# Context products of a cross-attention with high and low probabilities side by side, and the output weights' split one slot later

## What is computed

```python
q = rmsnorm((x @ Wq).reshape(b, s, 16, 128), gq)
k = rmsnorm((ctx @ Wk).reshape(b, 375, 16, 128), gk)
v = (ctx @ Wv).reshape(b, 375, 16, 128)
attn = softmax(einsum('bqhd,bkhd->bhqk', q, k) / sqrt(128))
out = einsum('bhqk,bkhd->bqhd', attn, v).reshape(b, s, 2048) @ Wo
```

## Time and profile before

| | |
|---|---|
| median of 3 runs | 1047.9 us |
| lowest and highest run | 1045.63 and 1049.46 us |
| profiled execution: its own time | 1046.03 us |
| profiled execution: span from first to last instruction | 1044.3 us |
| mean granted TensorE clock | 0.999 |

### The profile page before, as it was taken

The page is one execution under the profiler, slowest core; times in us unless marked ns, Lnnn a source line. Parts: engine busy times, 40 slices in busy tenths (PEclk is TensorE's granted clock), DMA queues, the critical chain, the costliest instruction groups (busy, mean ns, idle before and its releaser), DMA issues.

```text
span 1044.3 us, 20310 instructions
## 1 busy us (share of the span) xinstructions
PE 1018.9 (98%) x7021; PEld 910.0 (87%) x7021; DVE 722.6 (69%) x1496; ACT 536.6 (51%) x1075; POOL 532.7 (51%) x515
## 2 busy tenths in 40 slices
PE   8999999999999999999999999999999999999997
PEld 8856678999999999999999999999987888888885
DVE  4268876776767767767776776766886476666648
ACT  5355555555545455455555554554553356676610
POOL 1257767745534634643634634634474545544544
PEclk9999999999999999999999999999999999999999
DMA  8100114324333233323223233234220779999843
GB/s 279 83 32 2 61 39 153 143 109 157 116 108 114 99 107 111 101 109 116 96 111 115 94 117 109 98 118 136 98 90 1 286 282 386 387 393 399 294 119 113
DMA packets 45273, 153.46 MB, mean 147 GB/s; under 512 B 3768, under 2 KB 4792, under 8 KB 42144
## 3 DMA queue, kind: packets, MB, share of 16 engines
q1 hardware_dynamic: 42976, 145.38, 38.6%
q0 software_dynamic: 2240, 7.34, 2.1%
HBM read 130.04 MB, written 22.66 MB: 146 GB/s over the span
## 4 chain that ended last, share of the span: by engine, by line
PE 72%; POOL 5%; DVE 4%; issue 3%; ACT 1%; DMA 1%; POOLq 0%; DVEq 0%; ACTq 0%
PE xa_y_ps L86 6%; PE xa_y_ps L88 5%; PE xa_y_ps L87 5%; PE ex_raw_gu_ps L86 4%; PE ex_raw_gu_ps L88 4%; PE ex_raw_gu_ps L87 4%; PE xa_c_ps L1990 4%; PE xa_c_ps L1986 4%; PE xa_c_ps L1985 3%; PE ex_raw_ey_ps L2212 3%; PE xa_turn_ps L2067 3%; PE xa_turn_ps L2023 3%; PE front_k_ps L86 3%; PE front_k_ps L88 3%; PE front_k_ps L87 3%
## 5 line engine op out<-in xcount | busy, mean ns | idle before, releaser
L1300 POOL TENSOR_TENSOR xa_probs<-xa_probs,xa_inv_sum 112x750 f32<-112x750 f32 x63 | 97.9, 1553 | 75.5 <-DVE xa_inv_sum L1640 75.5
L1589 DVE TENSOR_TENSOR xa_kT_lo<-xa_turn_ps,xa_kT_hi 128x750 fp32r<-128x750 f32 x63 | 59.2, 939 | 99.9 <-ACT xa_kT_hi L1388 99.8
L1285 POOL TENSOR_TENSOR k_ms<-k_ss,sum_eps 125x6 f32<-125x6 f32 x63 | 12.6, 200 | 210.8 <-DVE k_ss L1605 210.8
L1985 PE MATMUL xa_c_ps<-xa_probsT_hi,xa_nat 125*128 125x224 f32 x384 | 92.3, 274 | 2.7 <-ACT xa_probsT_hi L1404 2.7
L1986 PE MATMUL xa_c_ps<-xa_probsT_hi,xa_nat 125*128 125x224 f32 x384 | 92.3, 275 | 0.0
L1404 ACT CAST xa_probsT_hi<-xa_turn_ps 125x672 fp32r<-125x672 f32 x62 | 44.6, 720 | 87.2 <-PE xa_turn_ps L2067 87.2
L1288 POOL TENSOR_TENSOR k_inv<-k_ms,neg_half 125x6 f32<-125x6 f32 x63 | 83.5, 1325 | 8.3 <-POOL k_ms L1285 6.7
L1410 ACT ACTIVATE xa_probs<-xa_scores_ps,xa_bias,xa_q_scale 112x375 f32<-112x375 f32 x126 | 82.8, 663 | 5.9 <-DVE xa_bias L1615 4.7
L1985 PEld LDWEIGHTS xa_c_ps<-xa_probsT_hi,xa_nat 125*128 125x128 f32 x384 | 73.6, 192 | 3.5 <-issue 3.1
L1986 PEld LDWEIGHTS xa_c_ps<-xa_probsT_hi,xa_nat 125*128 125x128 f32 x384 | 73.5, 191 | 0.5
L86 PE MATMUL front_k_ps<-land_xa_wk_hi,land_xa_ctx 128*125 128x256 f32 x252 | 71.4, 283 | 1.6 <-DVE front_k_hat L1632 1.2
(11 more groups left out here) (423 smaller groups left out, 3545.0 us busy)
## 6 DMA issues: line engine op xcount, KB each, us to landing
xa_nat<-ctx_split SPq DMA_DIRECT2D x56, 750.0 KB
ex_raw_raw<-in_w_units SPq DMA_DIRECT2D x15, 1408.0 KB, 8.2
ex_raw_raw<-in_w_units SPq DMA_DIRECT2D x15, 768.0 KB
land_ex_raw<-in_w_units SPq DMA_DIRECT2D x8, 1408.0 KB, 8.3
land_ex_raw<-in_w_units SPq DMA_DIRECT2D x8, 768.0 KB, 8.0
ctx_split<-xa_nat SPq DMA_DIRECT2D x8, 750.0 KB
sorted_x<-ex_raw_y_sb SPq DMA_DIRECT2D x7, 768.0 KB, 10.6
ex_raw_x_nat<-sorted_x SPq DMA_DIRECT2D x21, 256.0 KB, 8.6
```

The costliest lines, as they stand in the source:

```text
L1300: pool.tensor_tensor(probs[0:T, u % 2], probs[0:T, u % 2], inv_sum[0:T, u % 2, :].unsqueeze(2).broadcast_to([T, 2, KV]), ALU.mult).then_in ...
L1589: dve.tensor_tensor(kT_lo[:, :, 0:KV], turn_ps[:, :, 0:KV], kT_hi[:, :, 0:KV].bitcast(F32), ALU.subtract).then_inc(sem["kT_lo_done"], 1)
L1985: pe.matmul(c_view[:, c], nat[0:KT, u % 2, 0, at], probsT_hi[0:KT, :, cols], start=(t == 0), stop=False)
```

## The change

For batches u = 8 to 57 (`PAIRED`) high and low probabilities stand in one tile `probsT` beside each other, so that one matmul with nat high as weights takes both: 448 moving columns, of which 224 land in the first and 224 in the second half of a bank. Then three matmuls of 224 columns with nat low add to the first half. This takes a whole bank for each half c. The half c = 1 gets the second bank of `turn_ps`, in every paired batch; the half c = 0 has `c_ps` for itself in odd batches and is done so there, and in even batches stays as it was with nine matmuls ("three halves of four").

The sum of the two halves of a bank is now made late. ACT copies the first half as the high part (`cT_hi`, one copy for each c) and, for a paired half, the second half to `c_second`; DVE subtracts the high part from the first half into `c_rest`; POOL adds `c_rest` and `c_second` into `cT_lo`, as its first work in the slot. Since the second bank of `turn_ps` is used by the key transposes of the next slot, PE waits there, after the first keys, until DVE has read that bank (`second_bank_read`).

The output tile of each head pair's first sequence moves from slot 5 to slot 6 (`tile_of`), the rounding of the output weights moves on POOL behind `k_inv` of slot 4, their low part on DVE from the end of slot 4 to the start of slot 5, and the low part of the value weights on DVE from the end of slot 3 to the start of slot 4.

```diff
-        probsT_hi, probsT_lo = sb("probsT_hi", [P, 2, KT_N * T], F32R), sb("probsT_lo", [P, 2, KT_N * T], F32R)
+        probsT = sb("probsT", [P, 2, 2, KT_N * T], F32R)
+        probsT_hi, probsT_lo = probsT[:, 0], probsT[:, 1]
+        c_second = sb("c_second", [P, CC, 2, T])
+        c_rest = y_sb[:, 1, 0:CC * 2 * T].rearrange("p (c h t) -> p c h t", c=CC, h=2)
...
         def tile_of(u):
             b = u % B
-            return None if b == 1 else max(b - 1, 0)
+            return None if b == 0 else b - 1
...
+        c_pair = [bank[:, 0:4 * T].rearrange("p (l h t) -> p l h t", l=2, h=2) for bank in (c_ps, turn_ps[:, 1])]
+        PAIRED = range(B, N - B + 2)
+        def has_pair(u, c):
+            return c == 1 or u % 2 == 1
...
@@ POOL, slot @@
+                u = s - 3
+                if u in PAIRED:
+                    part = slice(u % 2 * T, (u % 2 + 1) * T)
+                    halves = slice(0 if has_pair(u, 0) else 1, CC)
+                    hold(pool, sem["c_rest_done"], i, CC * B, halves_read(u))
+                    pool.tensor_tensor(cT_lo[:, halves, :, part], c_rest[:, halves], c_second[:, halves],
+                                       ALU.add).then_inc(sem["cT_lo_done"], 1)
                 if s % B == 4 and s // B + 1 < PAIRS:
                     q = s // B + 1
                     split_hi(pool, i, q, "wq", wq_raw, wq_hi, "q_ready", 4, 4 * q)
...
-                if s % B == 4 and s // B < PAIRS:
-                    split_hi(pool, i, s // B, "wo", wo_raw, wo_hi, "y_ready", TILES, TILES * (s // B))
                 u = s
                 if u < N:
...
                     pool.tensor_tensor(k_inv[0:KT, :], k_ms[0:KT, :], env["neg_half"][0:KT, 0:2 * KT_N],
                                        ALU.pow).then_inc(sem["kinv_done"], 1)
+                if s % B == 4 and s // B < PAIRS:
+                    split_hi(pool, i, s // B, "wo", wo_raw, wo_hi, "y_ready", TILES, TILES * (s // B))
...
@@ ACT, slot @@
+                    for c in range(CC if u in PAIRED else 0):
+                        hold(act, sem["c_ready" if c else "c0_ready"], i, B, u + 1)
+                        act.copy(cT_hi[:, c, :, u % 2 * T:(u % 2 + 1) * T], c_pair[c][:, 0]).then_inc(sem["cT_hi_done"], 1)
+                        if has_pair(u, c):
+                            hold(act, sem["cT_lo_done"], i, B, u)
+                            act.copy(c_second[:, c], c_pair[c][:, 1]).then_inc(sem["c_second_done"], 1)
...
@@ DVE, slot @@
+                    for c in range(CC if u in PAIRED else 0):
+                        if has_pair(u, c):
+                            hold(dve, sem["c_second_done"], i, 3 * HALF, pairs_read(u, c))
+                            hold(dve, sem["cT_lo_done"], i, B, u)
+                        else:
+                            hold(dve, sem["cT_hi_done"], i, CC * B, CC * u + c + 1)
+                        dve.tensor_tensor(c_rest[:, c] if has_pair(u, c) else cT_lo[:, c, :, part], c_pair[c][:, 0],
+                                          cT_hi[:, c, :, part].bitcast(F32), ALU.subtract).then_inc(sem["c_rest_done"], 1)
+                if s % B == 4 and s // B < PAIRS:
+                    split_lo(dve, i, s // B, "wv", wv_raw, wv_hi, wv_lo)
+                if s % B == 5 and s // B < PAIRS:
+                    split_lo(dve, i, s // B, "wo", wo_raw, wo_hi, wo_lo)
...
-                if s % B == 3 and s // B < PAIRS:
-                    split_lo(dve, i, s // B, "wv", wv_raw, wv_hi, wv_lo)
-                if s % B == 4 and s // B < PAIRS:
-                    split_lo(dve, i, s // B, "wo", wo_raw, wo_hi, wo_lo)
...
@@ PE @@
+            def context_pairs(u, i):
+                context_loaded(u, i)
...
+                    hold(pe, sem["c_rest_done"], i, CC * B, halves_read(u - 1, 0))
+                hold(pe, sem["probsT_hi_done"], i, B, u + 1)
...
+                hold(pe, sem["probsT_lo_done"], i, B, u + 1)
+                for c in range(CC):
+                    if not has_pair(u, c):
+                        continue
+                    if c == 1:
+                        squares_taken(i, u + 2, 1)
+                    for t in range(KT_N):
+                        pe.matmul(c_pair[c], nat_part(u, 0, c, t), probsT[0:KT, :, :, cols[t]], start=(t == 0), stop=False)
+                    for t in range(KT_N):
+                        mm = pe.matmul(c_pair[c][:, 0], nat_part(u, 1, c, t), probsT_hi[0:KT, :, cols[t]], start=False,
+                                       stop=(t == KT_N - 1))
+                    mm.then_inc(sem["c_ready" if c else "c0_ready"], 1)
+            def second_bank_read(u, i):
+                hold(pe, sem["c_rest_done"], i, CC * B, halves_read(u))
...
@@ PE, slot: after the first keys, before the transposes of squares and keys @@
                     hold(pe, sem["probsT_lo_done"], i, B, u - 1)
                     squares_taken(i, s - 1, 1)
+                    if s - 3 in PAIRED:
+                        second_bank_read(s - 3, i)
                     turn_squares(i, s, 0)
```

More of the change, by code:

```diff
@@ L1577, in first_square_sums, with context_low @@
                                       ALU.add).then_inc(sem["qss_done"], 2)
+            def context_low(u):
+                part = slice(u % 2 * T, (u % 2 + 1) * T)
+                dve.wait_ge(sem["cT_hi_done"], CC * (u + 1))
+                dve.tensor_tensor(cT_lo[:, :, :, part], c_view, cT_hi[:, :, :, part].bitcast(F32),
+                                  ALU.subtract).then_inc(sem["cT_lo_done"], 1)
             def slot(s, i):
@@ L1581, in slot @@
                 if 0 <= u < N:
-                    hold(dve, sem["cT_hi_done"], i, B, u + 1)
                     part = slice(u % 2 * T, (u % 2 + 1) * T)
-                    dve.tensor_tensor(cT_lo[:, :, :, part], c_view, cT_hi[:, :, :, part].bitcast(F32),
-                                      ALU.subtract).then_inc(sem["cT_lo_done"], 1)
+                    if u not in PAIRED:
+                        context_low(u)
+                    for c in range(CC if u in PAIRED else 0):
[10 more added lines that the diff above has]
+                    split_lo(dve, i, s // B, "wo", wo_raw, wo_hi, wo_lo)
                 u = s - 1
@@ L1808, in combine @@
                                          in1=resid[:, t, :], op0=ALU.mult, op1=ALU.add).then_inc(xs["combined"], 1)
-            def context_low(u):
-                part = slice(u % 2 * T, (u % 2 + 1) * T)
-                dve.wait_ge(sem["cT_hi_done"], u + 1)
-                dve.tensor_tensor(cT_lo[:, :, :, part], c_view, cT_hi[:, :, :, part].bitcast(F32),
-                                  ALU.subtract).then_inc(sem["cT_lo_done"], 1)
             def probs_low(u):
@@ L1979, in context_of, with nat_part @@
                     hold(pe, sem[f"nat_{u % 2}_loaded"], i, 16 * HALF, 16 * (u // 2 - HALF + 1))
+            def nat_part(u, part, c, t):
+                return nat[0:KT, u % 2, part, t * CD + c * P:t * CD + (c + 1) * P]
+            def context_pairs(u, i):
+                context_loaded(u, i)
+                if u == B:
+                    pe.wait_ge(sem["cT_lo_done"], B)
+                else:
+                    hold(pe, sem["c_rest_done"], i, CC * B, halves_read(u - 1, 0))
+                hold(pe, sem["probsT_hi_done"], i, B, u + 1)
+                cols = [slice(t * T, (t + 1) * T) for t in range(KT_N)]
+                if not has_pair(u, 0):
+                    for t in range(KT_N):
+                        for part in range(2):
+                            pe.matmul(c_pair[0][:, 0], nat_part(u, part, 0, t), probsT_hi[0:KT, :, cols[t]],
+                                      start=(t + part == 0), stop=False)
+                    hold(pe, sem["probsT_lo_done"], i, B, u + 1)
+                    for t in range(KT_N):
+                        mm = pe.matmul(c_pair[0][:, 0], nat_part(u, 0, 0, t), probsT_lo[0:KT, :, cols[t]], start=False,
+                                       stop=(t == KT_N - 1))
+                    mm.then_inc(sem["c0_ready"], 1)
+                hold(pe, sem["probsT_lo_done"], i, B, u + 1)
+                for c in range(CC):
[3 more added lines that the diff above has]
+                        squares_taken(i, u + 2, 1)
+                    for t in range(KT_N):
+                        pe.matmul(c_pair[c], nat_part(u, 0, c, t), probsT[0:KT, :, :, cols[t]], start=(t == 0), stop=False)
+                    for t in range(KT_N):
+                        mm = pe.matmul(c_pair[c][:, 0], nat_part(u, 1, c, t), probsT_hi[0:KT, :, cols[t]], start=False,
+                                       stop=(t == KT_N - 1))
+                    mm.then_inc(sem["c_ready" if c else "c0_ready"], 1)
+            def second_bank_read(u, i):
+                hold(pe, sem["c_rest_done"], i, CC * B, halves_read(u))
+            def context_of(u, i):
+                context_loaded(u, i)
                 hold(pe, sem["cT_lo_done"], i, B, u)
```

33 lines of the change are left out of this document (20 added, 13 removed).

## The result

| | before | after |
|---|---|---|
| median of 5 runs each | 1048.26 us | 1041.21 us |
| lowest and highest run | 1045.63, 1049.46 | 1040.53, 1042.03 |
| profiled execution: its own time, span | 1046.03, 1044.3 | 1041.63, 1039.9 |
| mean granted TensorE clock | 0.999 | 0.999 |

The ratio is 0.9935 with a 95% interval of 0.992 to 0.9951, so the gain is clear of the noise. The forecast of 1043.6 us had the direction, and the time lies inside its range. By its bound of 0.5% it gave "the same" the larger chance, and the gain of 0.65% came out a little beyond that bound.

A forecast was written before the change was run, and what follows sets the result against it. PE bounds the kernel, by matmul count times spacing plus waits before weight loads. -4.8 + 0.3 - 2.5 + 2.7 = -4.3 us gives 1041.7 for the profiled execution; the median lies 1.9 above, so 1043.6 us, range 1039.8 to 1048.0.

The forecast's parts named there:

- the same: Whole kernel: a time within 0.5% (5.2 us) of no change; chance 0.53, against 0.38 for faster and 0.09 for slower.
- change 3: Output tile moved to slot 6: PE's 0.42 us stall for wo_lo in slot 5 goes in six head pairs, 2.5 us saved.
- change 4: POOL's order in slot 4: the addition meets wv_lo, k_hat makes PE 0.44 us late in six pairs, 2.7 us lost.
- change 1: Context products on PE: three 448-column matmuls replace six of 224 in 75 halves, 4.8 us saved.
- the loads' pace: Paired context products: weight loads of 107 ns set the matmul spacing, saving 74 ns a half, 5.5 us in all.
- the columns' pace: Paired context products: moving columns alone set the matmul spacing, 189 ns for 448 and 96 for 224, saving 0.6 us.
- Change 2: PE's new wait after the first keys for the second bank: due just when the wait ends, 0.3 us lost over 50 batches.
- The rival with both waits covered: Slot 4 and the second bank: POOL and DVE do not meet or meet the other way round, 1040.6 us; chance 0.2.
- The rival with a late second bank: PE's wait after the keys ends late, each 0.1 us costing 5 us, 1053.3 us at 0.2 late; chance 0.14.
- The wide matmul that saves nothing: Paired context products: 448 columns in four runs take 0.224 us each, +0.5 us in sum, 1048.4 us; chance 0.06.

The follow-up runs named there:

- e2: Changed kernel with POOL's addition of c_rest and c_second put behind the query weights in slot 4; median 1041.46 us, ratio 0.9912 to 0.9953 to the kernel before.
- e3: Changed kernel with DVE's low part of the value weights back at the end of slot 3; median 1041.95 us, ratio 0.9923 to 0.9961 to the kernel before.
- e1: Kernel before with only the moves of output tile, output-weight rounding and DVE's low parts, products unpaired; median 1043.15 us, ratio 0.9939 to 0.9975.
- e4: Changed kernel with one more ACT copy of 128 columns before the c = 1 copy to c_second; median 1046.02 us, ratio 0.9984 to 1.0009 to the kernel before.
- e5: Changed kernel with DVE's low part of the output weights back at the end of slot 4; 1059.92 us in one execution.
- e8: Kernel before with only the paired products; tile, rounding and both low parts in their old places; 1060.91 us in one execution.
- e0: Kernel before, run again unchanged; median 1047.14 us, ratio 0.9975 to 1.0002.
- e9: Changed kernel, run again unchanged, beside the kernel before on one chip; median 1042.02 us against 1047.71, ratio 0.9931 to 0.9964.
- e6: Changed kernel with the first 3 of 12 query matmuls of slot 5 moved ahead of the scores; median 1039.02 us, ratio 0.9914 to 0.9947 to the kernel before.

## Why the prediction was right, and where its sizes were off

The mechanism was right: the same four terms, each with its sign, make the result. The stage became 5.5 us shorter where the sum said 4.3; change 3 gave 1.1 more than summed and change 4 cost 0.5 less, and change 1 gave 0.5 less.

- **Change 1, -4.8: measured -4.3.** In the median the product takes 1.890 in odd and 1.952 in even batches against 2.007, so 25 x 0.117 + 25 x 0.055 = 4.3. Right in kind; the first wide matmul of a half is spaced by 0.21, not 0.20. By the Trainium skill ("TensorE: Matmul & The Clock Gate", sections "LDWEIGHTS" and "Back-to-back issue gap") the loads' pace gave an estimate of 5.5 us and the columns' pace, which the second of these sections gives for an isolated matmul, one of 0.6. The trace's 4.3 lies nearer the first; that the loads set the pace no run here tests.
- **Change 2, +0.3: measured 0.1 to 0.3.** The pairing without the stall for `k_hat` is e2 or e3 less e1, -4.0 and -4.2 us, so of the -4.3 some 0.1 to 0.3 is lost. In the slots s % 8 = 4 and 0 the load of the first transpose starts 0.16 and 0.15 us after the last key's, where in the others and in the kernel before it is 0.13: some 0.3 us in all, for which the trace names no cause. That the wait is level was right, and e4 shows what 0.08 us in it costs. One reading under it was wrong: the 0.035 by which `kT_hi` starts before the ACT instruction ahead ends is not what two ready instructions overlap by, because `kT_hi` was released only then (last section).
- **Change 3, -2.5: measured -2.7 for `wo_lo` and -0.6 beside it.** The stall went, and its counterpart moved without growing: `wo_lo` was done before `kT_hi`. The prediction took 0.42 for six pairs; e1's seven waits add up to 2.75. What the step failed to count is the rounding behind `k_inv` in the first two pairs. The move is worth 3.6 us, and the 0.3 that the idle loads do not account for is not explained.
- **Change 4, +2.7: measured +2.1 to +2.3.** (6 x 0.44 is 2.64, so the prediction's own figure was 2.6.) The instants differ from those worked out because all of slot 4 lies earlier after the change, but the chain is the one given: an addition of 1.53 (forecast 1.50), six stalls at the head of slot 5 of 0.35 and 0.42 in the pair's length (forecast 0.44).

The rival with both waits covered (1040.6) is nearer to the median than the forecast is, and still not what happened: its `k_hat` wait is there, 2.1 us. It describes e2 and e3. The rival with a late second bank did not come true, but e4, e5 and e8 show how near it was, and that DVE's place for `wo_lo` decides it. The wide matmul that saves nothing is ruled out by the spacing.

What separates 7.05 from 5.5 us is most likely the scatter of the stage behind the gathers: the profiled execution of before, against which the sum was made, had that stage at 42.2 us, e0 had it at 46.1, and the medians of before came out between 1046.15 and 1048.58 with nothing changed. In e9's set the difference is 5.7. The prediction scaled the sum to a median of three runs without asking which stage made them differ.

## What to carry to other kernels

Take the length of the changed stage from the trace as the measure, and check by a second profile of the same kernel which stages repeat: here one repeated within 0.15 us and another moved by 4. When a change adds a wait that is just met, look for what stands ahead on each engine of its chain, since the place of one weight split on DVE decided between 5.5 us gained and 11.6 lost (e5, of which some 2.6 are the clock's). And the stall that a piece of work covered, and that shows when the work is moved away, is itself a place for independent work (2.5 us in e6).

## What the hardware showed beyond that

**ACT's copies overlap by more than counted.** The second of two 224-column copies starts 0.24 us after the first, which is 0.34 long: 0.10 of overlap. The Trainium skill ("ScalarE: Activation LUTs", section "What ACT_TABLE_LOAD costs") has about 0.093 for activations back to back; the trace agrees. The prediction took 0.035 from `kT_hi` of the earlier trace rows, which starts at 361.37. The transposes that it copies end at 361.33 in the kernel before, so it started when its input was there:

```profile
360.53 0.80 PE L2023 MATMUL xa_turn_ps<-ident,front_k_hat 125*128 125x125 f32 x6
```

**The clock falls in some runs after an idle PE, and not in others.** Two head pairs of e5, the slot with the 2.4 us stall, in the view of windows:

```profile
348.52:360.86 12.34, 9.93 (x64) 8.85 (x64) 9.30 (x16) 5.83 (x14) 7.47 (x8) 1.00 0.34 117
429.79:442.98 13.19, 10.98 (x64) 10.28 (x65) 9.30 (x16) 5.89 (x14) 7.46 (x8) 0.87 0.33 111
```

The same 64 matmuls take PE 1.05 us more at a mean granted clock of 0.87, so for a part of the second stretch the clock was at the lower of its two levels, 1.2 GHz; the slot is 0.85 us longer. The kernel after and e9 are one program. Behind the last keys PE's weight loads stand idle in front of the context products in both, for 1.05 us and again for 0.61 (after) and 0.66 (e9). The stretch that follows, in the kernel after and in e9:

```profile
769.00:775.00 6.00, 6.00 (x46) 5.63 (x45) 4.29 (x8) 3.65 (x8) 5.13 (x4) 1.00 0.26 92
```

```profile
769.00:775.00 6.00, 6.00 (x37) 5.63 (x37) 3.48 (x6) 1.84 (x3) 5.26 (x3) 0.82 0.17 60
```

At 0.82 PE did 37 matmuls in 6 us instead of 46, and e9 reached the experts 1.6 us later. What decides whether the clock falls in a given run stays open.
